# Second feed-forward: the shared experts' output tiles made two abreast, their 64-row last chunks on different halves of TensorE's rows

## The reference, cut to what matters

```
h = layernorm(x)                              # 4096 tokens x 512
# 64 routed experts, top 6 of the softmax of h @ gate_w.T, at most 64 tokens each:
y = sum over chosen experts of  w * ((silu(h @ w_gate[e]) * (h @ w_up[e])) @ w_down[e])
# shared experts, inner width 2 * 352 = 704 = 5 * 128 + 64:
shared = (silu(h @ sw_gate) * (h @ sw_up)) @ sw_down
x = x + y + shared
```

## Time and profile before

| what | us |
|---|---|
| median of three runs | 3288.41 |
| profiled execution: its time, its span | 3294.18, 3292.4 |
| PE, DVE, POOL, ACT busy | 2838.2, 1785.2, 1542.7, 1281.2 |
| second feed-forward, front: first `turn` to first `up` | 2381.1 to 2814.0 |
| second feed-forward, experts: first `up` to the end | 2814.0 to 3292.4 |
| first feed-forward, experts: first `up` to the last add landed | 1216.1 to 1670.5 |
| mean duration of DVE's `hid` on 128 x 512 and on 64 x 512 | 0.69, 0.69 |

### The profile page before, as it was taken

The page is one execution under the profiler, slowest core; times in us unless marked ns, Lnnn a source line. Parts: engine busy times, 40 slices in busy tenths (PEclk is TensorE's granted clock), DMA queues, the critical chain, the costliest instruction groups (busy, mean ns, idle before and its releaser), DMA issues.

```text
span 3292.4 us, 38105 instructions
## 1 busy us (share of the span) xinstructions
PE 2838.2 (86%) x13772; PEld 1516.4 (46%) x13772; DVE 1785.2 (54%) x3715; ACT 1281.2 (39%) x2673; POOL 1542.7 (47%) x949
## 2 busy tenths in 40 slices
PE   4668888778888879888868999999799899999998
PEld 2445545544555434333335555555444443444443
DVE  5898897989889942212235666665324344222221
ACT  4556566555656511101116666667412121011111
POOL 6998798978879802121226555555200000212212
PEclk7669999988999989999979999999899999999999
DMA  5443453535345369999930000000234220899997
GB/s 183 141 164 129 161 187 122 191 108 191 134 161 174 134 226 339 346 344 345 330 118 1 27 27 27 27 14 14 103 112 146 93 74 21 292 350 331 345 347 196
DMA packets 199053, 557.67 MB, mean 169 GB/s; under 512 B 25040, under 2 KB 26960, under 8 KB 198352
## 3 DMA queue, kind: packets, MB, share of 16 engines
q1 hardware_dynamic: 181168, 514.19, 44.9%
q0 software_dynamic: 16640, 39.86, 5.4%
q10 hardware_dynamic: 1056, 1.18, 0.1%
HBM read 480.42 MB, written 74.74 MB: 169 GB/s over the span
## 4 chain that ended last, share of the span: by engine, by line
PE 55%; DVE 13%; POOL 12%; DMA 8%; ACT 5%; issue 4%; SPq 3%; POOLq 0%; DVEq 0%; ACTq 0%
PE bank L976 9%; PE bank L1037 7%; PE bank L943 6%; PE bank L964 6%; POOL arena L1717 6%; DMA arena<-in_w_up 4%; PE bank L1084 4%; PE bank L1141 3%; POOL arena L1723 3%; PE bank L1063 3%; PE bank L1118 3%; DVE arena L1222 3%; DVE bank L1222 2%; PE bank L885 2%; PE bank L915 2%
## 5 line engine op out<-in xcount | busy, mean ns | idle before, releaser
L1717 POOL TENSOR_TENSOR arena<-arena 128x1024 f32<-128x1024 f32 x256 | 613.2, 2396 | 90.6 <-PE bank L915 77.9
L1575 ACT ACTIVATE bank<-arena 128x512 f32<-128x512 f32 x512 | 344.1, 687 | 409.5 <-DVE arena L1222 295.5
L915 PE MATMUL bank<-arena 128*128 128x128 f32 x2048 | 308.4, 303 | 181.4 <-POOL arena L1723 181.0
L1806 POOL TENSOR_TENSOR arena<-arena 128x2048 f32<-128x2048 f32 (+3 forms) x128 | 296.8, 2321 | 277.8 <-DVE arena L1443 277.8
L915 PEld LDWEIGHTS bank<-arena 128*128 128x128 f32 x2048 | 260.2, 156 | 264.6 <-POOL arena L1723 216.0
L976 PE MATMUL bank<-arena 128*128 128x512 f32 (+1 forms) x768 | 360.5, 613 | 15.1 <-DVE arena L1245 15.1
L1638 ACT ACTIVATE arena<-arena 128x256 f32<-128x256 f32 (+3 forms) x512 | 286.2, 562 | 201.7 <-DVE arena L1434 171.5
L1222 DVE TENSOR_TENSOR_SCAN arena<-bank,arena 128x512 f32<-128x512 f32 x256 | 311.1, 1215 | 67.8 <-ACT bank L1575 45.4
L1723 POOL TENSOR_TENSOR arena<-arena 128x512 f32<-128x512 f32 x256 | 326.8, 1277 | 33.6 <-DVE arena L1222 32.9
L1037 PE MATMUL bank<-arena 128*64 128x352 f32 x2048 | 328.6, 475 | 0.0
L1222 DVE TENSOR_TENSOR_SCAN bank<-bank,arena 128x512 f32<-128x512 f32 x256 | 308.5, 1205 | 0.0
(11 more groups left out here) (134 smaller groups left out, 4196.0 us busy)
## 6 DMA issues: line engine op xcount, KB each, us to landing
arena<-scratch_bc SPq DMA_DIRECT2D x128, 1024.0 KB, 5.4
arena<-in_w_gate SPq DMA_DIRECT2D x128, 704.0 KB
arena<-in_w_up SPq DMA_DIRECT2D x128, 704.0 KB
arena<-in_w_down SPq DMA_DIRECT2D x128, 512.0 KB
arena<-in_w_down SPq DMA_DIRECT2D x128, 192.0 KB
scratch_x<-arena SPq DMA_DIRECT2D x16, 1024.0 KB, 4.5
scratch_xn<-arena SPq DMA_DIRECT2D x15, 1024.0 KB, 8.6
arena<-scratch_x SPq DMA_DIRECT2D x48, 256.0 KB, 5.9
```

Of the source, the lines that this page charges most:

```text
L915: i = nc.tensor.matmul(y[:, t * P:(t + 1) * P], w[:, n, t * P:(t + 1) * P], p.ident, is_transpose=True, start=False, stop=g == GROUPS - 1 ...
L1575: nc.scalar.activation(bank[p.da_bank(k, n)][:, :], block_of(p.dt, b, c), ACT.Exp, scale=p.alog[:, c, state:state + 1]).then_inc(*p.decaye ...
L1717: nc.gpsimd.tensor_tensor(out=p.hb[k % HB], in0=over(block_of(p.dtx, b, c), 1, NG), in1=p.bc[k // 2 % NBC][:, 0], op=ALU.mult).then_inc(*p ...
L1806: nc.gpsimd.tensor_tensor(out=own, in0=own, in1=over(p.rden[:, k % 2, :], 2, width), op=ALU.mult).then_inc(*p.divided.up(k))
```

## The change

`ABREAST = (1, 2)` gives the number of output tiles made together, 2 in feed-forward 1. There an output unit now holds two tiles. PE does the five full chunks of the first tile into its bank, the five of the second into the next bank, and then the two 64-row chunks one behind the other: the even tile's from rows 64 to 127, the odd tile's from rows 0 to 63. For that the last 64 rows of `sw_down` are loaded twice, into both halves, and the last `hid` is two instructions, one for the even tiles' columns and one, which writes rows 0 to 63, for the odd ones'. The units are counted anew: `size` counts a unit of two tiles as 2, but `spend(n)` takes whole units until n is used up, so it can take one more than n. In feed-forward 0 the instructions and the plan stay as they are.

```diff
+ABREAST = (1, 2)
+def last_rows(m, t):
+    return slice(0, LAST_S) if t % ABREAST[m] else slice(P - LAST_S, P)
+def every(step, n, ap):
+    return ap.rearrange("p (i s c) -> p i s c", s=step, c=P)[:, :, n, :]
...
-        for t in range(QT):
-            u = [("fetch", m, q, t + 1)] * (t < QT - 1) + [("sd", m, q, t), ("so", m, q, t)]
+        for t in range(0, QT, ABREAST[m]):
+            tiles = range(t, t + ABREAST[m])
+            u = [("fetch", m, q, n + 1) for n in tiles if n < QT - 1]
+            u += [("sd", m, q, n) for n in tiles] + [("so", m, q, n) for n in tiles]
...
+    def left(self):
+        return sum(map(self.size, self.units))
+    def size(self, unit):
+        return sum(i[0] in ("hid", "so") for i in unit)
     def spend(self, n):
...
+            n -= self.size(self.units[-1])
             out += self.units.pop()
-            n -= 1
...
-            plan += units.spend(len(units.units) - left * (NPAIR - 1 - p) // NPAIR)
+            plan += units.spend(units.left() - left * (NPAIR - 1 - p) // NPAIR)
...
-        for j in range(SC):
-            rows = slice(0 if j < SC - 1 else P - LAST_S, P)
-            i = nc.tensor.matmul(out[:, :], f["shT"][rows, j, t * P:(t + 1) * P], f["swd"][rows, j, :],
-                                 start=j == 0, stop=j == SC - 1)
-        i.then_inc(*ring.made.up("sd", m, q, t))
+        for j in range(SC - 1):
+            nc.tensor.matmul(out[:, :], f["shT"][:, j, t * P:(t + 1) * P], f["swd"][:, j, :], start=j == 0, stop=False)
+        if (t + 1) % ABREAST[m]:
+            return
+        for n in range(t + 1 - ABREAST[m], t + 1):
+            rows = last_rows(m, n)
+            nc.tensor.matmul(bank[ring.bank("sd", m, q, n)][:, :], f["shT"][rows, SC - 1, n * P:(n + 1) * P],
+                             f["swd"][rows, SC - 1, :], start=False, stop=True).then_inc(*ring.made.up("sd", m, q, n))
...
+            for n in range(ABREAST[m]):
+                i = nc.vector.tensor_tensor(out=every(ABREAST[m], n, out[last_rows(m, n), :]),
+                                            in0=every(ABREAST[m], n, gate), in1=every(ABREAST[m], n, up), op=ALU.mult)
...
-        nc.sync.dma_start(f["swd"][P - LAST_S:, SC - 1, :], d["sw_down"][whole:, :]).then_inc(*p.shared_w.up(m, 3))
+        for t in range(ABREAST[m]):
+            nc.sync.dma_start(f["swd"][last_rows(m, t), SC - 1, :], d["sw_down"][whole:, :]).then_inc(
+                *p.shared_w.up(m, 3 + t))
```

More of the change, by code:

```diff
@@ L443, in expert_plan @@
     plan = [("xturn", m, 0), ("gather", m, nx)]
-    left = len(units.units)
+    left = units.left()
     for p in range(NPAIR + 1):
@@ L748, in semaphores @@
         self.gate_w = sig("gate_w", "ff_w", by=16)
-        self.shared_w = sig("shared_w", "ff_w", parts=range(4), by=16)
+        self.shared_w = Signal(self, "shared_w", [(m, n) for m, in self.keys("ff_w") for n in range(3 + ABREAST[m])], 16)
         self.xn_out = sig("xn_out", "xn_out", by=16, where=lambda m, q: (m, q) != LAST_BESIDE)
@@ L936, in shared_gate @@
         turned = p.ring_of(("F", m, q))
-        PE.wait_ge(p.shared_w, m, 3)
+        PE.wait_ge(p.shared_w, m, 2 + ABREAST[m])
         PE.wait_ge(turned.taken_by["act"], "turn", ("F", m, q), HC - 1)
@@ L1238, in hidden @@
         gates = p.ring_with("sg", m, q, j)
-        n = P if j < SC - 1 else LAST_S
-        rows = slice(P - n, P)
         V.wait_ge(gates.taken_by["act"], "sg", m, q, j)
@@ L1244, in hidden @@
             V.wait_ge(p.ring_with("sd", m, q - 1, QT - 1).made, "sd", m, q - 1, QT - 1)
-        nc.vector.tensor_tensor(out=f["shT"][rows, j, :], in0=f["ssg"][rows, :],
-                                in1=bank[ring.bank("su", m, q, j)][rows, :],
-                                op=ALU.mult).then_inc(*ring.taken_by["dve"].up("su", m, q, j))
+        gate, up, out = f["ssg"], bank[ring.bank("su", m, q, j)], f["shT"][:, j, :]
+        if j < SC - 1:
+            i = nc.vector.tensor_tensor(out=out, in0=gate, in1=up[:, :], op=ALU.mult)
+        else:
+            gate, up = gate[P - LAST_S:, :], up[P - LAST_S:, :]
+            for n in range(ABREAST[m]):
+                i = nc.vector.tensor_tensor(out=every(ABREAST[m], n, out[last_rows(m, n), :]),
+                                            in0=every(ABREAST[m], n, gate), in1=every(ABREAST[m], n, up), op=ALU.mult)
+        i.then_inc(*ring.taken_by["dve"].up("su", m, q, j))
     def shared_out(m, q, t):
```

## The result

The changed kernel takes 3314.86 us (median of six runs, 3301.24 to 3323.66), against 3289.19 for the kernel before in runs of its own beside it. The ratio is 1.0072, with a 95% interval of 1.0045 to 1.01: slower by about 24 us. The forecast was 3313, slower, with a range of 3286 to 3323.

A forecast was written before the change was run, and what follows sets the result against it. PE was taken to bound the second feed-forward's front, and DMA its experts' part after the change. Front +33.5 and experts -8.4 us gave +25, on the 3288.41 median 3313 us, range 3286 to 3323.

The forecast's parts named there:

- The bound of each stage: Second feed-forward: PE bounds the front; the experts' part has PE and DMA full, and after the change DMA alone bounds it.
- The pairing: Output tiles: two 64-row matmuls on different row halves overlap fully, so a pair costs 9.84 us, not 11.08, saving 1.24.
- (a) to (d): Front up to the last fold: more projection units +31.0, output tiles -2.6, outputs' waits +2.8, clock -1 us.
- (c): Front: outputs' waits for a quad's last `hid`, two new ones of 4.9 us, 17.2 in all instead of 14.4: +2.8.
- (d): Front: less half-speed clock behind waits, -1 us, bounds -6 and +4.
- (e): Front behind the last fold: 13.7 instead of 10.4 us of work behind `lists`, hidden by nothing: +3.3 us.
- Front in sum: Second feed-forward's front, to the first `up`: longer by 33.5 us, bounds 26 to 40.
- Experts' stage: Second feed-forward's experts' part: 470.0 us instead of 478.4, a gain of 8.4, bounds 2 and 17.
- 8.5 us for a later end: End of the experts' part: the last two outputs come together, lengthening the chain of adds; last add issued 8.5 us later.
- experts bound by PE: Rival, chance 0.12: DMA can exceed 340 GB/s, so the experts' part shrinks by 43.8 us and the total is 3278.
- The front takes it in: Rival, chance 0.19: no new waits in the front, clock falls less often, no later end; +9.5 us, total 3298.
- Pairs don't overlap: Rival, chance 0.07: 64-row matmuls in different halves run one behind the other; front pairs cost +9.2 us, total 3323.

The follow-up runs named there:

- e4: Changed kernel loading only half of the gate and up weights from the sixth expert on in the second feed-forward (output differs): 3273.82 us, ratio 0.9946.
- e2: Changed kernel's plan, but each output tile made by itself with its own 64-row chunk, one load and one `hid`: 3332.61 us, ratio 1.0124.
- e3: Changed kernel's plan and matmul order, but both 64-row chunks of a pair on the same half of PE's rows: 3328.12 us, ratio 1.0104.
- after_again: The changed kernel run once more, unaltered, beside the others: 3317.05 us, ratio 1.0086 to the kernel before.
- e5: Changed kernel with the experts' stage's remaining outputs all placed by pair 21 of 32, not pair 28; same front: 3311.67 us, ratio 1.0055.
- e1_again: Repeat of the changed kernel with pairs kept but `spend`'s overshoot carried over, so units split between front and experts' stage as before: 3280.24 us, ratio 0.9958.
- e7: Changed kernel with no unit asked for behind a fold (3, 3, 0); four projections and one output pair move to the experts' stage: 3311.26 us, ratio 1.0065.
- e9: e7 with one projection put back behind the last fold only, as many units in front: 3312.37 us, ratio 1.005.
- e8: Unit counts of e1_again, but the changed kernel's plan up to the third fold, five units fewer behind it: 3280.45 us, ratio 0.9973.
- e10: e8 with the last outputs of the experts' stage at pair 26 instead of 29: 3281.24 us, ratio 0.997.

## Why the prediction was right

- **The bound of each stage**: right, though PE was busier in the experts' stage than forecast (92%, not near 85%). e4 shows it for the transfers of the experts' stage, and e2 for PE in the front.
- **The pairing**: 9.84 predicted, 9.81 and 9.84 measured. The choice of full overlap, drawn from the 32-row scores, is what e3 confirms.
- **(a) to (d), up to the last fold**: +30.2 predicted (31.0 - 2.6 + 2.8 - 1). Measured from `turn` to fold: 418.3 (2787.52 - 2369.2) against 389.0 (2770.12 - 2381.1), +29.3.
- **(c) alone**: two new waits at quads 1 and 4, predicted 4.9 each, measured 4.3 and 4.25; all waits of the outputs 17.2 predicted, 15.2 measured, so +0.8 and not +2.8. The -1 for the clock (d) must then have been some 1 us too low: two small errors partly cancelled.
- **(e)**: +3.3 predicted. Fold to first `up` is 46.1 now against 43.8, +2.2.
- **Front in sum**: +33.5 predicted, +31.6 measured (464.4 against 432.8), +32.3 in after_again.
- **Experts' stage**: 470.0 predicted, 465.7 and 469.1 measured.
- **Inside that sum one term is mis-sized.** The 8.5 us for a later end exists behind the last `up` (e5 takes 8.7 away), but most of it returns ahead of it, and the stage keeps only 1 to 4. In e5, where the term is gone, my sum gives 454.4 + 3.3 + 3.8 = 461.5, and the stage lasted 464.9. So some 3 us of the stage are not in my list, and the mis-sized term covered for them, which is luck; 3 us is also what the stage differs by between two executions (465.7 and 469.1), so what they are stays open.
- **The sum**: +25 predicted. The stages give +31.6 - 12.8 = +18.8 and +32.3 - 9.4 = +22.9 in the two profiles; the medians differ by 25.7 and 21.9. Of the runs, which spread from 3301 to 3324, the median falls within 2 us of the forecast; that close a hit is luck.
- **The rivals**: "experts bound by PE" would have had the stage fall by 43.8; it fell by 9 to 13 and the rate stayed at 343 GB/s. The Trainium skill, "HBM Reference", section "Specifications (TRN2)", has a lone core measure about 425 GB/s; no run here shows it for this mix. Stretches of 10 us do reach 400 GB/s ahead of the first experts' stage of before (1160 to 1170), but over the 400 us of an experts' stage the rate stays at 340 to 343. "The front takes it in" failed on the waits, which did form. "Pairs don't overlap" is e3.

One thing was not in the prediction: PE waits 0.7 us for the last part of `sw_down` ahead of the front's first projection. It is not tied to the second load: e2, with one load, waits 0.3 us, and e1_again, with two, not at all.

## What to carry to other kernels

A planner that counts units changes the schedule when a unit grows. Here that side effect cost 37 to 41 us and hid a gain of 11 to 13, and it took four lines to undo: compare the plans of before and after by stage before judging the edit itself. Work that fills a stage bound by transfers is nearly free there (PE's busy time in it fell from 460 to 412 and 418 us, and that won 9 to 13) and costs its full length wherever PE is the bound, as in the front (+29.3 us up to the fold). When filler moves, ask both what wait it covered and which queue its followers join: as the traces of e7 and e9 read, an add that a moved tile hands to POOL held back the gather that everything waited for.

## What the runs showed of the hardware

- Two float32 matmuls of 64 rows on different halves of PE's rows, each into its own bank, take 1.06 us in all with the change of shape, on the same half 1.91, and a single one 1.05.
- Execution to execution, code that is identical differs by several us: the first `turn` of the second front lies at 2369.2 in after and 2374.0 in after_again, and equal fronts took 424.0 and 417.2 us. The half clock in the outputs behind a wait of 4 to 10 us cost 1.7 to 3 us (10.52, 11.27 and 11.33 us behind 4.3, 11.8 behind 9.7, for 8.82); here are two such, of e8 and of e10, at the same place of the program, with a granted clock of 0.78 and 0.84:

```profile
2505.13 11.33 PE L996 MATMUL bank<-arena 128*128 128x512 f32 x20 [4.31 <-DVE arena L1273]
2498.76 10.52 PE L997 MATMUL bank<-arena 128*128 128x512 f32 x20 [4.30 <-DVE arena L1274]
```

- An indirect add that waits for the one before takes mostly 9 to 10.5 us from issue to issue while the weights stream (11.9 at most in after), and 5.6 us without them.
